# A new order of steps in the attention loop of a fused attention and expert kernel

## The reference

```
n   = layernorm(x)
q   = n Wq^T + bq;   k = ctx Wk^T + bk;   v = ctx Wv^T + bv        # 16 heads of 16
s   = q k^T / 4, masked keys to -1e9;  p = softmax(s)
x   = x + (p v) Wo^T + bo
xf  = layernorm(x);  xa = xf P_w^T
Ci  = softmax of the 3 largest of xa Ui^T, else 0                  # i = 1, 2, 3; 12 experts
h   = gelu(sum_e C1[:, e] * (xf W1[e]^T))
x   = x + sum_e C2[:, e] * (h W2[e]^T) + C3 b2
```

## Time and profile before

| | |
|---|---|
| median of 3 runs | 412.53 us (411.24 to 412.81) |
| profiled execution | 412.67 us, span of its instructions 410.9 us |
| mean granted TensorE clock | 0.988 |
| busy: PE, PEld, DVE | 392.6 us (96%), 333.4 (81%), 341.1 (83%) |
| busy: ACT, POOL | 115.8 us (28%), 110.9 (27%) |
| DMA moved | 12.71 MB, mean 31 GB/s |

### The profile page before, as it was taken

How to read it: one execution, slowest core, us unless ns; L and a number is a source line. 1 busy time by engine, 2 the same in 40 slices (tenths; PEclk the granted TensorE clock), 3 DMA queues, 4 the chain that set the end, 5 groups by cost and what they waited for, 6 DMA issues and landing times.

```text
span 410.9 us, 7824 instructions
## 1 busy us (share of the span) xinstructions
PE 392.6 (96%) x2132; PEld 333.4 (81%) x2132; DVE 341.1 (83%) x1036; ACT 115.8 (28%) x263; POOL 110.9 (27%) x165
## 2 busy tenths in 40 slices
PE   4699999999989999999999999999999999999996
PEld 4479889898878788888888888888888888888884
DVE  3788898898895889798898978989788898888875
ACT  3467888888921211010101101011010101101000
POOL 5462647466540211202022020211202022020200
PEclk9889999999989999999999999999999999999999
DMA  7900131222000000000000000000000000000000
GB/s 228 331 0 3 52 102 54 99 87 66 2 0 2 1 2 14 13 0 13 0 13 0 13 13 0 13 0 13 13 0 13 0 13 3 10 13 0 14 0 26
DMA packets 8612, 12.71 MB, mean 31 GB/s; under 512 B 1076, under 2 KB 5016, under 8 KB 8472
## 3 DMA queue, kind: packets, MB, share of 16 engines
q1 hardware_dynamic: 8040, 12.44, 9.2%
q10 hardware_dynamic: 560, 0.13, 0.1%
HBM read 10.47 MB, written 2.10 MB: 31 GB/s over the span
## 4 chain that ended last, share of the span: by engine, by line
PE 87%; DVE 4%; issue 3%; ACT 3%; POOL 1%; DMA 1%; ACTq 0%; POOLq 0%; DVEq 0%
PE banks L920 67%; PE banks L997 4%; PE banks L987 3%; PE banks L962 2%; PE banks L972 2%; PE banks L975 2%; PE banks L977 2%; PE banks L1035 1%; DVE q_hl L625 1%; DMA bk_sb<-in_bk_dram 1%; PE banks L1043 1%; PE banks L1025 1%; ACT w_h L534 1%; PE banks L1008 1%; POOL w_l L366 1%
## 5 line engine op out<-in xcount | busy, mean ns | idle before, releaser
L815 DVE SCALAR_TENSOR_TENSOR s_d<-banks,c_cur,s_d 128x256 f32<-128x256 f32 x165 | 72.6, 479 | 25.2 <-PE banks L920 22.2
L920 PE MATMUL banks<-w_h,xf_h 128*128 128x512 f32 x204 | 81.8, 401 | 0.0
L920 PE MATMUL banks<-w_l,xf_h 128*128 128x512 f32 x204 | 80.3, 394 | 0.0
L920 PE MATMUL banks<-w_h,xf_l 128*128 128x512 f32 x204 | 80.2, 393 | 0.0
L406 POOL TENSOR_TENSOR top_e<-euler,top_d 128x9 f32<-128x9 f32 x16 | 28.9, 1806 | 183.2 <-DVE top_d L765 183.2
L920 PE MATMUL banks<-w_h,h_h 128*128 128x512 f32 x180 | 73.0, 406 | 0.0
L920 PE MATMUL banks<-w_l,h_h 128*128 128x512 f32 x180 | 70.5, 392 | 0.0
L920 PE MATMUL banks<-w_h,h_l 128*128 128x512 f32 x180 | 70.1, 390 | 0.0
L815 DVE SCALAR_TENSOR_TENSOR sum<-banks,c_new,sum 128x256 f32<-128x256 f32 x160 | 66.2, 478 | 3.1 <-PE banks L920 3.1
L561 ACT ACTIVATE h_h<-banks 128x256 fp32r<-128x256 f32 x15 | 5.8, 384 | 153.8 <-PE banks L1043 153.8
L920 PEld LDWEIGHTS banks<-w_l,xf_h 128*128 128x128 f32 x204 | 38.7, 190 | 8.4
(11 more groups left out here) (126 smaller groups left out, 624.3 us busy)
## 6 DMA issues: line engine op xcount, KB each, us to landing
stage<-in_w_t_dram SPq DMA_DIRECT2D x12, 512.0 KB, 3.6
out_dram<-x_all SPq DMA_DIRECT2D x16, 128.0 KB, 1.9
x_all<-in_x_dram SPq DMA_DIRECT2D x1, 1024.0 KB, 7.3
x_all<-in_x_dram SPq DMA_DIRECT2D x1, 768.0 KB, 7.9
mask_all<-in_mask_dram SPq DMA_DIRECT2D x2, 256.0 KB, 5.0
x_all<-in_x_dram SPq DMA_DIRECT2D x2, 128.0 KB, 3.8
wk_sb<-in_wk_t_dram SPq DMA_DIRECT2D x1, 256.0 KB, 3.7
wq_sb<-in_wq_t_dram SPq DMA_DIRECT2D x1, 256.0 KB, 4.5
```

Source lines behind the costliest of these rows:

```text
L815: dve.scalar_tensor_tensor(out=sums[e % 2][:, :], in0=product, scalar=weights[:, e:e + 1], in1=sums[e % 2][:, :], op0=ALU.mult, op1=ALU.ad ...
L920: ins = pe.matmul(dst, a(c), b(c), start=(i == 0), stop=(i == len(terms) - 1))
```

## The change

`normalise1` runs one tile further ahead on DVE than before. POOL and SP are as they were. The diff, cut to its core:

```diff
 # ScalarE
-            def q_high(t):
+            def q_biased(t):
                 act.wait_ge(q_done, t + 1)
...
                     nc.scalar.activation(q[:, c, :], ps_q[:, c, :], ACT.Identity,
                                          bias=bq_sb[:, c:c + 1]).then_inc(q_copied, 1)
+
+            def q_high(t):
                 act.wait_ge(q_copied, C * t + C)
...
+            q_biased(0)
             q_high(0)
             copy_xt(1)
+            q_biased(1)
             q_high(1)
+            copy_xt(2)
             exp_scores(0)
-            copy_xt(2)
+            q_biased(2)
+            copy_pt(0)
+            q_high(2)
             (wo_h)
+            copy_xt(3)
+            exp_scores(1)
             (b2_hhl, three instructions)
-            copy_pt(0)
-            q_high(2)
-            exp_scores(1)
-            copy_xt(3)
-            def attention(t):
-                copy_pt(t)
-                a_high(t - 1)
-                q_high(t + 2)
-                exp_scores(t + 1)
+            def attention(t, g=None, r=None):
+                q_biased(t + 2)
+                if r is not None:
+                    split_weights(g, r)
+                a_high(t - 1)
+                copy_pt(t)
+                q_high(t + 2)
+                if not isinstance(t, int) or t < T - 3:
+                    copy_xt(t + 3)
+                exp_scores(t + 1)
 # VectorE
             normalise1(3)
             q_low(2)
+            stats1(4)
             (router_w)
             divide_by_sum(0)
-            stats1(4)
+            normalise1(4)
...
-            def attention(t):
+            def attention(t, ahead=True):
                 max_scores(t + 1)
                 subtract_max(t + 1)
+                if ahead:
+                    stats1(t + 4)
                 a_low(t - 1)
-                normalise1(t + 3)
                 q_low(t + 2)
                 divide_by_sum(t)
                 add_attention(t - 1)
+                if ahead:
+                    normalise1(t + 4)
...
-            attention(T - 4)
+            attention(T - 4, ahead=False)
 # TensorE
             transpose_x(2)
+            queries(2)
             scores(1, 0)
             transpose_probs(0)
-            queries(2)
+            transpose_x(3)
             weigh_values(0, 0)
-            transpose_x(3)
-            def attention(t, b, b_next):
+            def attention(t, b, b_next, ahead=True):
+                queries(t + 2)
                 scores(t + 1, b_next)
+                transpose_a(t - 1)
                 transpose_probs(t)
-                transpose_a(t - 1)
-                queries(t + 2)
+                if ahead:
+                    transpose_x(t + 3)
                 weigh_values(t, b)
                 output_project(t - 1)
```

More of the change, by code:

```diff
@@ L534, in split_weights @@
                 nc.scalar.activation(w_h[:, g * RING + r, :, :], stage[:, r, :, :], ACT.Copy).then_inc(w_hi, 1)
+            def attention(t, g=None, r=None):
[8 more added lines that the diff above has]
+                exp_scores(t + 1)
             attention(1)
-            copy_xt(4)
             with act.Fori(0, CHUNKS // RING - 1) as g:
                 for r in range(RING):
-                    attention(g * RING + (r + 2))
-                    split_weights(g, r)
-                    copy_xt(g * RING + (r + 5))
+                    attention(g * RING + (r + 2), g, r)
             for r in range(RING):
[L545 to L548, removed]
+                attention(T - 2 - RING + r, CHUNKS // RING - 1, r)
             copy_xf(0)
@@ L733, in attention @@
                 add_attention(t - 1)
+                if ahead:
+                    normalise1(t + 4)
             attention(1)
-            stats1(5)
             dve.wait_ge(x_in[3], 16)
@@ L739, in _ @@
                 attention(t)
-                stats1(t + 4)
-            attention(T - 4)
+            attention(T - 4, ahead=False)
             statistics(0, x_all, bn2_done, stats2_ready)
@@ L1106, in _ @@
             attention(1, 0, 0)
-            transpose_x(4)
             pe.wait_ge(kbd_set, 3)
@@ L1112, in _ @@
                 attention(t, t // TPB, (t + 1) // TPB)
-                transpose_x(t + 3)
-            attention(T - 3, BATCH - 1, BATCH - 1)
+            attention(T - 3, BATCH - 1, BATCH - 1, ahead=False)
             transpose_xf(0)
```

## The result

| | before | changed |
|---|---|---|
| median | 412.46 us (7 runs, 411.18 to 412.88) | 415.19 us (7 runs, 414.27 to 416.48) |
| ratio, 95% interval | 1 | 1.0087 (1.0069 to 1.0105) |
| profiled execution, its span | 412.67, 410.9 us | 415.89, 414.2 us |
| mean granted clock | 0.988 | 0.992 |

The change costs 0.87%, 2.7 us of the medians and 3.2 us of the profiled executions. 415.4 was forecast, with a range of 411.0 to 419.5. Where the time went shows in the windows first (columns as in the earlier trace rows).

A forecast was written before the change was run, and what follows sets the result against it. TensorE, nearly always busy, was the bound; the change would close a circle through the engines at 6.90 us a body. +6.2 - 1.75 - 1.55 = +2.9 us on 412.67 gives 415.6, median 415.4, range 411.0 to 419.5.

The forecast's parts named there:

- Parts 1 and 2: Attention loop: queries first ends the scores wait; statistics ahead of a_low make a circle of 6.90 us a body, against 6.41.
- The sign that I named: Attention loop: TensorE's largest wait is the output product for a_low, about 0.5 us, 11 times.
- The other signs: No scores wait for q_hl; bodies 6.9 us apart, last two shorter; one slow stretch near 27 us; xf_low 0.415.
- What queries first could gain: Attention loop: removing the scores wait for q_low brings at most about 0.3 us a body; a body's work is 6.1.
- Part 3: Attention loop: the new ACT and POOL order, including the place of split_weights, is worth nothing.
- Part 4: Prologue: TensorE idles about 2.3 us, then a half-clock stretch costs 1.5 us; scores(3) comes 2.1 us later.
- Part 5: Bodies 2 to 13: 6.9 us each, 6.4 from body 12; scores(15) at 118.1 against 111.93, +6.2 us in all.
- Part 6: Transition to the experts: xf_low no longer beside w_l gives -1.75 us, full clock afterwards -1.55 us.
- The sum: Whole kernel: +6.2 - 1.75 - 1.55 = +2.9 us on the profiled execution's 412.67 us.
- A: Rival, attention loop: a_low is not late, the body stays 6.4 us, time 409.9; chance 0.14.
- C: Rival, attention loop: idle time in the bodies brings slow-clock stretches, +8 us, time 423; chance 0.08.
- B: Rival, attention loop: POOL's work blocks q_low, up to 0.3 us a body, time 417.1; chance 0.10.

The follow-up runs named there:

- e1: Changed kernel with the statistics stats1(t+4) moved behind a_low(t-1) on DVE: 411.64 us, ratio 1.0008 to the kernel before.
- e10: e3 with ACT's split_weights ahead of the attention body instead of behind it: 409.20 us, ratio 0.9945 to the kernel before.
- e7: e6 with transpose_probs ahead of transpose_a on TensorE and copy_pt ahead of a_high on ACT: 408.66 us, ratio 0.9929.
- e9: e8 with POOL's rstd of tile 4 ahead of wo_l and DVE's b2_hhl step behind body 1: 407.46 us, ratio 0.9903.
- e3: Kernel before with only DVE's new order, TensorE and ACT keeping the old one: 438.58 us, ratio 1.0658.
- e8: e7 with ACT's rounding of wo_h moved behind exp_scores(1): 410.53 us, ratio 0.9964 to the kernel before.
- e5: Changed kernel with weigh_values(0) put back ahead of transpose_x(3) in TensorE's prologue: 415.31 us, ratio 1.0072 to the kernel before.
- e4: Kernel before with POOL's inverse_deviation(1) ahead of its last w_l subtraction, moving that off xf_low(0): 408.83 us, ratio 0.9926.
- e6: Changed kernel with the statistics behind a_low and weigh_values(0) ahead of transpose_x(3): 410.34 us, ratio 0.9976 to the kernel before.

## Why the prediction was right

**The body (Parts 1 and 2): right in kind and nearly in size.** 6.90 forecast (6.78 to 7.01), 6.79 measured. The one link that differs is from the second statistics instruction to `a_low`: I took 0.22 between 0.10 and 0.33, and 0.10 is what it is, the lower of the two rows. e1 shows that with the statistics behind it `a_low` is no longer late. The sign that I named, about 0.5 us of wait for `a_low` 11 times as TensorE's largest in the loop, did not show: between 20 and 126 us TensorE's list has 0.2 us in one place for it and 2.5 us in 13 places for `prob_t`, because `weigh_values`, by its modelled end, covers most of the 0.3 us. The other signs came: no wait for `q_hl`, and the last two bodies shorter (6.56 and 6.72).

What queries first could gain I had too high. I took the work of a body for 6.1 us and the gain for 0.3, but by the earlier trace rows TensorE is busy 69.31 us in 11 bodies, 6.30 each, and the shortest bodies of any run are 6.26 (e10) and 6.29 us (e7, e9).

**ACT and POOL at nothing (Part 3): right for the changed kernel**, whose body is the sum of the circle without them. But e3 and e10 show that, with the old order on TensorE, the new place of `split_weights` is worth 29 us: a move priced at zero can be one that the others need. What it is worth with queries first no run shows.

**The prologue (Part 4): right in kind, too small.** +2.1 us forecast, +3.5 measured (`scores(3)` at 38.21 against 34.74). The hole was there, 2.09 us where I had put 2.3, but the slow stretch began at once, under `weigh_values(0)`, and lasted about 6.8 us (25.7 to 32.5), where the one of before lasted 3.3. This term, 1.5 us, was too small. Body 1 started at 28.49 instead of 27.6 and took 8.83 us instead of 8.4:

```profile
25.17 1.93 DVE L627 TENSOR_TENSOR q_hl<-q,q_hl 64x256 fp32r<-64x256 f32 x2
...
25.20 0.44 PE L957 MATMUL banks<-ident,xn 128*128 128x128 f32 x2 [2.09 <-DVE xn L604]
...
25.47 3.21 PE L1001 MATMUL banks<-v_ext,prob_t 128*128 128x34 f32 x16
25.55 1.27 POOL L386 TENSOR_TENSOR wo_l<-wo_sb,wo_h 128x512 fp32r<-128x512 f32 x1 [0.81 <-ACT wo_h L519]
...
28.49 2.06 PE L966 MATMUL banks<-xn_t,wq_sb 128*128 128x128 f32 x8
```

`weigh_values(0)` took 3.0 us (25.47 to 28.49) instead of 1.71. I had also seen `wo_l` move away from `normalise1` and not that it came to lie under the step behind, `q_low(2)`: 1.93 us instead of 0.85. It cost nothing here, since `scores(2)` came at 30.34. By the rule of the Trainium skill (SBUF — State Buffer, "SBUF: two separate sides") a VectorE step with two SBUF inputs is shut out while a GpSimd instruction that reads SBUF and started first runs. The trace agrees, here in the second half of `q_low(2)`, and in e8, where 0.85 us came back once `wo_l` lay elsewhere. And the hole was not the prologue's only limit, as e5 showed: without it DVE holds body 1 back (TensorE stands 1.71 us for `a_low(0)`), and a slow stretch follows all the same.

**To the last scores (Part 5):** +6.2 forecast, +6.55 measured (118.48 against 111.93): 1.3 more from the prologue, 1.1 less from ten bodies, and 0.2 more from body 12 (6.56 us where I had 6.4).

**The transition (Part 6): right.** -1.75 and -1.55 forecast, -1.73 and -1.60 measured, and e4 shows both alone.

**The sum:** 6.55 - 1.73 - 1.60 = 3.2 us, the difference of the profiled executions, where 2.9 was forecast. Two errors of over one microsecond, the body's and the prologue's, had opposite signs. That the number came out within 0.3 us is therefore partly luck; the mechanisms of the body and of the transition are not.

**The rivals.** A (a body of 6.4) fell: `a_low` was late. C fell: PEclk is 1.00 in the ten bodies with TensorE at 65.29 of 67.88 us. B cost nothing in the changed kernel: one `q_low` is longer there, 1.11 us at 110.59, and no `scores` waits for it. But its mechanism is real, as e10 shows.

## What to carry to other kernels

When a step is put ahead of another on an engine that works in order, draw the circle through all engines back to itself; each instruction in it costs its time in each round, however idle its engine is, down to the length of the next path. Here 0.56 us of statistics cost 0.29 us a body (6.79 against 6.50). Then ask of each engine's queue what stands ahead of the value that the circle needs: in e3 a `rstd` of half a microsecond, behind a 2.4 us subtraction that itself waited for the last step on ScalarE, cost 29 us. A hole in TensorE's work of 1.5 to 2 us may be paid twice, the second time in half clock, and closing it helps only if the next engine in line is ready too.

## What was not expected of the hardware

The clock's reaction to a similar hole is not the same each time. e5, e6, e7, e8 and e9 all have TensorE busy 1.33 of the 1.80 us from 25.2 to 27.0. In e6 and e7 the granted clock then is 0.50 from 27 to 30, in the three others 1.00; of these e5 and e8 have a slow stretch from about 35 on. e7:

```profile
25.20:27.00 1.80, 1.33 (x11) 1.09 (x11) 1.75 (x3) 1.61 (x3) 1.26 (x1) 0.98 0.00 0
27.00:30.00 3.00, 3.00 (x13) 2.45 (x12) 2.59 (x9) 1.94 (x6) 1.79 (x5) 0.50 0.02 5
```

The same window of e9, above, has 1.00. The changed kernel and e1 are a second such pair: behind the hole of 2.1 us at the same step, 1.7 us later in e1, the one has half clock for about 6.8 us, the other 1.00. There is also a slow stretch ahead of those that I had read. The kernel before has a clock of 0.50 from 14 to 16 us, and e1 has 0.51 from 15 to 20, but the changed kernel's profiled execution has 1.00 from 10 to 25.2. In the kernel before it costs nothing, since `scores(1)` starts at 20.62, and at 20.67 in the changed kernel; in e1, where it is longer, `scores(1)` starts at 22.40.

So the slow stretch of Part 4 is worth about 1.5 us of uncertainty (an estimate, from its price in the prediction) that the profile of one execution doesn't remove. Only the profiled run has a trace, but each run has its mean clock. e9's profiled run, 406.44 us, has 0.996, its four others, 407.40 to 407.64 us, have 0.991 to 0.994: they had more half clock than the trace shows, and where it lay can't be seen.

The lock between DVE and POOL takes from either side. In e10 it stretches `q_low` from 0.85 to 1.33 us, where POOL's bias addition starts under its first half; in the changed kernel, where the addition starts under the second half (`q_low` from 43.27, the addition from 43.77), it is the addition that takes 0.97 us instead of 0.73.
